# Weight splits, a context split and a low part put at other places in the queues of a decoder layer's first stage

## The reference

```python
x = x + attn(layernorm(x), Wq, Wk, Wv, Wo)              # 32 heads, 8 key heads, head size 16, rope, causal
x = x + xattn(layernorm(x), ctx, Wq, Wk, Wv, Wo, ...)   # 32 heads of 128, 8 key heads, keys of ctx and latents
x = x + linear(layernorm(x), 4-bit weights) + bias
```

## Time and profile before

| | |
|---|---|
| median of 3 runs | 974.43 us (974.26 to 975.17) |
| profiled execution | 974.2 us, its span 972.4 us |
| TensorE busy | 921.2 us (95% of the span) |
| VectorE, ScalarE, GpSimd busy | 738.6, 608.0, 560.2 us (76, 63, 58%) |
| mean granted TensorE clock | 0.984 of full speed |
| first part | to about 207.7 us of the span |

### The profile page before, as it was taken

One profiled execution on the slowest core, in us unless ns is written; L12 is line 12 of the kernel. 1 busy time (PEld: TensorE's weight loads), 2 busy tenths in 40 slices (PEclk: granted clock), 3 DMA queues, 4 the chain that ended last, 5 costly groups with the idle time before them and its releaser, 6 DMA issues.

```text
span 972.4 us, 17522 instructions
## 1 busy us (share of the span) xinstructions
PE 921.2 (95%) x5488; PEld 792.8 (82%) x5496; DVE 738.6 (76%) x1556; ACT 608.0 (63%) x2229; POOL 560.2 (58%) x591
## 2 busy tenths in 40 slices
PE   6799988688999999999999999999999999999987
PEld 5677776467888888888888888888888888888776
DVE  6698888737777777777777777777777777788985
ACT  4688877527666665676657566656656675556541
POOL 6333224216945785575568656856774586558742
PEclk8999999789999999999999999999999999999999
DMA  5000200017765576556655665665576446654531
GB/s 206 13 12 22 77 13 13 0 55 250 223 214 165 173 233 211 173 167 204 203 174 186 211 213 153 210 220 169 165 234 206 153 154 219 209 169 150 158 129 55
DMA packets 101164, 149.84 MB, mean 154 GB/s; under 512 B 11856, under 2 KB 77392, under 8 KB 98896
## 3 DMA queue, kind: packets, MB, share of 16 engines
q1 hardware_dynamic: 101072, 148.71, 47.9%
HBM read 87.85 MB, written 60.82 MB: 153 GB/s over the span
## 4 chain that ended last, share of the span: by engine, by line
PE 71%; DVE 4%; ACT 2%; POOL 2%; issue 1%; DVEq 0%; POOLq 0%
PE ps_kv L73 18%; PE ps_y L73 17%; PE ps_q L73 17%; PE ps_o L73 8%; PE ps_s L73 8%; ACT ps_s L1119 1%; POOL pT_raw L1038 1%; PE ps_f L73 1%; DVE neg_max L1219 0%; DVE p L1231 0%; DVE p_blocks L1235 0%; DVE kT_lo L1258 0%; DVE f_stats L1294 0%; DVE x L1265 0%; POOL qT_lo L1031 0%
## 5 line engine op out<-in xcount | busy, mean ns | idle before, releaser
L1119 ACT ACTIVATE ps_s<-ps_s,bias,q_rms 128x256 f32<-128x256 f32 x256 | 136.8, 535 | 139.6 <-DVE bias L1223 139.6
L1031 POOL TENSOR_TENSOR qT_lo<-qk_raw,qT_hi 128x512 fp32r<-128x512 f32 x64 | 84.5, 1320 | 203.0 <-ACT qT_hi L1148 203.0
L1038 POOL TENSOR_TENSOR pT_raw<-pT_raw,pT_hi_sb 128x1024 fp32r<-128x1024 f32 x63 | 151.5, 2405 | 5.8 <-ACT pT_hi_sb L1142 5.6
L1136 ACT ACTIVATE q_squares<-ps_q 128x128 bf16<-128x128 f32 x256 | 67.4, 278 | 112.0 <-DVE qk_blocks L1253 112.0
L73 PE MATMUL ps_y<-wo_hi,oT_hi 128*128 128x512 f32 x252 | 100.0, 397 | 3.9 <-DVE oT_lo L1269 3.9
L73 PE MATMUL ps_q<-wq_lo,xT_hi 128*128 128x512 f32 x256 | 101.4, 396 | 0.0
L1235 DVE STREAM_TRANSPOSE p_blocks<-p 128x512 f32<-128x512 f32 x128 | 91.0, 711 | 13.3
L73 PE MATMUL ps_q<-wq_hi,xT_lo 128*128 128x512 f32 x256 | 101.1, 395 | 0.0
L73 PE MATMUL ps_q<-wq_hi,xT_hi 128*128 128x512 f32 x256 | 100.9, 394 | 0.0
L73 PE MATMUL ps_y<-wo_lo,oT_hi 128*128 128x512 f32 x252 | 99.5, 395 | 0.0
L73 PE MATMUL ps_y<-wo_hi,oT_lo 128*128 128x512 f32 x252 | 99.4, 394 | 0.0
(11 more groups left out here) (233 smaller groups left out, 2928.3 us busy)
## 6 DMA issues: line engine op xcount, KB each, us to landing
p_scratch<-p_blocks SPq DMA_DIRECT2D x64, 512.0 KB, 3.0
pT_raw<-p_scratch SPq DMA_DIRECT2D x256, 128.0 KB, 3.0
qk_scratch<-qk_blocks SPq DMA_DIRECT2D x64, 384.0 KB, 3.5
qk_raw<-qk_scratch SPq DMA_DIRECT2D x256, 96.0 KB, 3.0
raw_wq<-in_x_wq SPq DMA_DIRECT2D x8, 1024.0 KB, 8.0
raw_wo<-in_x_wo SPq DMA_DIRECT2D x8, 1024.0 KB, 7.7
raw_wkv<-in_x_wkv SPq DMA_DIRECT2D x8, 512.0 KB, 5.1
ctx_raw<-in_ctxT SPq DMA_DIRECT2D x8, 256.0 KB, 2.6
```

The lines of the kernel that those rows point to most:

```text
L1031: pool.tensor_tensor(qT[1][:].rearrange("p g (i c) -> p g i c", i=4), qk_raw[s % 2][:, :, 0:XG, :].rearrange("p i g c -> p g i c"), f32(qT ...
L1038: pool.tensor_tensor(raw, f32(raw), f32(pT_hi_sb[:].rearrange("p i t x -> p (i t x)")), ALU.subtract).then_inc(pT_lo, 1)
L1119: e = act.activation(scores, scores, ACT.Exp, bias=bias[:, g:g + 1], scale=q_rms[:, s % 4, g:g + 1], accum_out=total[:, g:g + 1])
L1136: i = act.activation(q_squares[:, g, :], ps_q[:, g * XD:(g + 1) * XD], ACT.Square, scale=XD ** -0.5, accum_out=q_mean[:, g:g + 1])
```

## The change

It moves six steps of the first part and adds one wait. On GpSimd the queries are rotated right after the keys; context's split follows, and for rows 1 to 7 it waits until the queries' low part is made; the two subtractions of the first head's weights stand together behind the last context. On VectorE the low part of the next x goes ahead of the key tiles (the call at n = -1 keeps its place); the cast of the key-value weights goes behind the spread and the last transposed probabilities of row 6, the cast of the query weights from row 7 to the end of row 6's list.

```diff
--- before.py
+++ after.py
@@ -282,12 +282,14 @@
             for m in range(1, B + 2):
                 if m < B:
                     rotate_keys(m)
+                    rotate_queries(m)
                 if m <= B:
+                    if m < B:
+                        pool.wait_ge(q_lo, m + 1)
                     context(m - 1)
-                if m < B:
-                    rotate_queries(m)
-                if m >= B:
-                    cross_weights_low(m - B)
+                if m == B:
+                    cross_weights_low(0)
+                    cross_weights_low(1)
                 if m >= 2:
                     rstd_2(m - 2)
 
@@ -541,16 +543,15 @@
                     queries_low(n + 1)
                 if now:
                     probs_transposed(n, 2)
+                if later:
+                    xn_low(n + 2)
                 if n == -1:
-                    xn_low(1)
                     dve.wait_ge(x_in, 16)
                     statistics(range(2, B))
                 if after:
                     key_tiles(n + 1)
                 if now:
                     maxima(n, 5)
-                if later and now:
-                    xn_low(n + 2)
                 if n >= 1:
                     statistics_2(n - 1)
                 if now:
@@ -558,13 +559,11 @@
                     probs_transposed(n, 4)
                 if n >= 1:
                     normalised_2(n - 1)
+                if now:
+                    inverse_totals(n)
+                    probs_transposed(n, 5)
                 if n == B - 2:
                     cross_weights_high(0)
-                if n == B - 1:
-                    cross_weights_high(1)
-                if now:
-                    inverse_totals(n)
-                    probs_transposed(n, 5)
                 if n == -1:
                     maxima(0, 0)
                     maxima(0, 1)
@@ -587,6 +586,8 @@
                     output_low(n)
                 if after:
                     maxima(n + 1, 2)
+                if n == B - 2:
+                    cross_weights_high(1)
             dve.wait_ge(norm_in, 32)
             dve.scalar_tensor_tensor(mem["key_scale"][:], norm_w[:, 0:1], float(XD) ** -0.5, norm_w[:, 1:2],
                                      ALU.mult, ALU.mult).then_inc(scale_ok, 1)
```

More of the change, by code:

```diff
@@ L560, in _ @@
                     normalised_2(n - 1)
-                if n == B - 2:
-                    cross_weights_high(0)
-                if n == B - 1:
-                    cross_weights_high(1)
                 if now:
@@ L567, in _ @@
                     probs_transposed(n, 5)
+                if n == B - 2:
+                    cross_weights_high(0)
                 if n == -1:
```

## The result

The median is 963.16 us (961.0 to 964.1, 4 runs) where the kernel before has 974.8 (974.26 to 977.81, 4 runs): a ratio of 0.9871, 95% interval 0.9845 to 0.9897, so 1.3% faster. The forecast was 962.4 with 960.3 to 965.6. The profiled execution took 963.0 us, its span 961.2. Some lines have moved by a few numbers: the spread copy is L462 now, the casts L498, the low part of the next x L397, TensorE's spread transposes L720.

A forecast was written before the change was run, and what follows sets the result against it. TensorE's idle time in the first stage, waiting for the low part of x and the spreads of rows 6 and 7, was the bound; 1.7 + 0.5 + 3.0 + 0.8 + 4.6 + 1.4 = 12.0 us gave 962.4, range 960.3 to 965.6.

The forecast's parts named there:

- Low part of the next x: Rows 0 to 5: moved ahead of the key tiles, it shortens each row by 0.28 us, 1.7 us in all.
- row 0's rotation: Row 0 on GpSimd: the queries' rotation no longer stands behind context, 0.5 us gained once.
- Spread of row 6: Row 6: without cast and weights' subtraction, the spread's transposes start at 168.27 instead of 171.23, 3.0 us gained.
- Stretch to the output projection: Row 6, from spread transposes to output projection: 7.70 us at 1.2 GHz, half the possible clock gain taken, 0.8 us.
- Spread of row 7: Row 7: no cast or subtraction at the spread, TensorE goes on at 188.45 instead of 193.09, 4.6 us gained.
- Stretch of row 7: Row 7's spread to the next stage's first product: 3.11 us becomes 1.68 with the clock up, 1.4 us gained.
- Hidden parts: Context's wait, the moved casts and the second subtraction: expected to be covered by idle time and cost about nothing.
- The second part shifts whole: The second stage starts when the first is over and was taken to move earlier without changing length.
- The range: Forecast's own range by the ends 960.4 to 964.0 us; the wider one, with the clock's rival, to 965.6.
- the clock's: Rival: TensorE's clock falls to 1.2 GHz in both stretches, losing 0.8 and 1.4 us; 964.6 us, chance 0.20.
- the other two: Rivals: row 6's spread covered by a later context, 966.2 us, chance 0.06; slower through context delaying roots, chance 0.03.
- four signs of being wrong: Granted clock 0.50 after either spread, VectorE waiting for a root, a longer second stage, row pitch still 19.98.

The follow-up runs named there:

- e1: Kernel before with one edit alone, the low part of the next x ahead of the key tiles: 973.1 us, ratio 0.9979.
- e2: Kernel before with GpSimd's edit alone, queries rotated ahead of context and context waiting for the queries' low part: 974.47 us, ratio 0.9991.
- e4: Kernel after with GpSimd's subtraction of the query weights put back behind row 6's root, the cast staying moved: 968.48 us.
- e5: Kernel after without the added wait of context for the queries' low part: 963.73 us.
- e3: Kernel before with the weights' edits alone, casts behind the spreads and both subtractions together on GpSimd: 965.31 us, ratio 0.9892.
- e6: Kernel after with the maxima of a row's last unit ahead of the next row's key tiles on VectorE: 955.89 us.
- e7: Kernel after with 30 unread transposes on TensorE, 12 behind the first part and 18 ahead of the second part's loop: 964.12 us.
- e8: Kernel after with both the maxima moved ahead of the key tiles and the 30 unread transposes at the joint: 955.2 us.

## Why the prediction was right

It was right in its sum and, within half a microsecond, in each term of the first part; its step from there to the second part failed, and one term came near partly by luck.

- **Low part of the next x, 1.7, and row 0's rotation, 0.5.** Together 2.2 predicted, 2.21 measured up to row 6. That they agree so closely is chance: row 0's rope, ahead of every edit's effect, stands 0.34 us later in this profile (35.32 against 34.98), so the edits gave 2.55. The pitches from row 1 to row 6 give 0.28 to 0.31 each, as said; from row 0's rope to row 1's q_stack it is 1.12 where the sum had 0.78, and there TensorE's wait for the low part had been the longest of the six, 1.59 us. The pitch of 19.70 and e1's 19.71 bear out the choice of the row that has no next x over the wait's full 1.20 us. e2 bears out the 0.5 up to row 6; its rope stands at 35.00.
- **Spread of row 6, 3.0.** 2.97. Context's subtraction became the cover of the copy, as said, and the copy took the 1.1 us named. The prediction took the copy's end as the bound; the scores ahead of the transposes end 0.09 later, so either would have given the 3.0.
- **Stretch to the output projection, 0.8.** 0.75. The clock fell again, after the 2.22 us wait, and came back under way. But the half was a middle between two ends and not worked out, and that it came so near is luck in part: with the spread freed the same stretch takes 6.57 us in e4, 6.95 here and in e5, and 7.33 to 7.38 in e3, e6, e7 and e8, where the spread runs at the upper clock (0.66 us) and the clock falls behind it. Against the 7.70 of before that is a gain of 0.3 to 1.1.
- **Spread of row 7, 4.6.** 4.94. I let the spread start when the transposes ahead of it end (0.60 us); TensorE starts it 0.44 after they start (182.22 - 181.78), which is 0.16 of the rest. The other 0.14 lies ahead of them: from the output projection to them it is 8.78 us now and was 8.92, with the first product at 0.48 instead of 0.60.
- **Stretch of row 7, 1.4.** 1.43, at the upper clock throughout.
- **Hidden parts.** Context's wait, the casts' new places and the second subtraction's new place were costed at nothing, and nothing shows: no wait for a root or for context stands in TensorE's list, and e5 without the wait is the same.
- **The second part shifts whole.** This was the one step that failed: it is 1.1 us longer (8.48 against 7.34 us for its first products). The text put some drift of the clock there into the range, not into the sum. Less the 0.3 us by which the terms came out larger, it makes the 0.8 us between the forecast's 962.2 for the profiled execution and its 963.0.
- **The range.** The 960.4 to 964.0 called the forecast's own don't follow from the ends named: the two stretches' ends alone (0 to 1.7 and 0 to 1.4) give 961.5 to 964.6. The range on record, 960.3 to 965.6, holds both.

Of the rivals, the clock's came half true (0.51 in the two microseconds after row 6's spread, 1.00 after row 7's); the other two find nothing in the trace. So two of the prediction's four signs of being wrong came: a low clock after a spread, and a longer second part. The first cost nothing against the sum, which had only half of that stretch's gain in it; the second cost the 1.1 us.

What stays open is why the clock at the joint came back later in the work, with the same wait of 4.1 us ahead. It isn't chance alone: in the four kernels in which TensorE still waits 3.2 to 4.6 us in row 7 (before, e1, e2, e4) the first 36 products take 7.34 to 7.40 us, in the four without that wait and without the idle transposes (the kernel after, e3, e5, e6) 8.39 to 8.49. How the one leads to the other no run shows. From the start of the second part to its first residual the profiles show 44.75 us before, 44.79 in e1, 44.83 in e4, against 45.88 in the kernel after, 45.99 in e3, 46.40 in e5 and 46.04 in e6; e2 is apart with 46.68, though its first products are quick. From that residual to the end all ten profiles take 719.8 to 720.0 us, so this drift of up to 2 us is all that the second part scatters. The first part's scatter lies in its start-up: row 0's q_stack stands between 36.24 us (e4) and 39.41 (e7).

## What to carry to other kernels

When a short VectorE copy reads many times its usual length, look at what GpSimd runs at that moment: if both work in SBUF and the copy starts and ends just after GpSimd's operation, move the long operation to where VectorE reads PSUM, and check what else of VectorE it then meets (e4's normalisation). A wait's length is no measure of its worth: the next one behind it is, and a row of the same kernel that lacks the wait shows it (1.20 us of wait, 0.28 of gain). And after a gain, read the list of waits again: the one that took its place here fell to two swapped lines (e6), worth more than half as much as the whole change.

## What was not expected

- The exclusion catches VectorE's normalisation too, an operation with one SBUF tensor and two columns of scalars: 4.61 us beside GpSimd's subtraction, 0.54 without.
- What a blocked operation has left when GpSimd ends goes by its columns: 0.28 us for 512, 0.54 for 1024, and 1.09 for 1024 with two SBUF inputs (e5).
- Keeping TensorE's clock up at the joint moved its fall and gave nothing back: at 1.00 through the joint in e7, it fell about the next wait, 2.7 us for the probabilities, and the six and 24 products behind it took 1.5 us more than in the kernel after (6.06 against 4.54).
